# Four places instead of two for the split parts of queries and keys in a fused two-layer transformer kernel

## The reference, cut to what matters

```
xh = x[:, :, :DH];  x1 = layernorm(xh + mha(xh, wq1, ...), g1, be1)
xs = holt(x, 0.1, 0.1); x2 = layernorm(xs[:, :, :DH] + mha(xs[:, :, :DH], wq2, ...), g2, be2)
q = x @ wq.T + bq;  k = x @ wk.T + bk;  v = x @ wv.T + bv      # 8 heads of 8
a = softmax(q k^T / sqrt(8));  o = a v
```

## Time and profile before

| what | value |
|---|---|
| time, median of 3 runs | 2137.68 us (2133.76 to 2138.3) |
| profiled execution | 2140.73 us, span of its trace 2138.9 us |
| TensorE busy | 1884.9 us, 88% of the span |
| VectorE busy | 1776.4 us, 83% |
| ScalarE busy | 1444.4 us, 68% |
| GpSimd busy | 344.0 us, 16% |
| first `lead` (block 0) starts | 47.77 us |
| `lead` of blocks 2 to 7 starts | 62.86, 72.05, 81.15, 90.26, 99.48, 108.59 us |
| L730 starts | 117.37 us |
| first row maximum (L758) starts | 139.84 us |

### The profile page before, as it was taken

The page is one execution under the profiler, slowest core; times in us unless marked ns, Lnnn a source line. Parts: engine busy times, 40 slices in busy tenths (PEclk is TensorE's granted clock), DMA queues, the critical chain, the costliest instruction groups (busy, mean ns, idle before and its releaser), DMA issues.

```text
span 2138.9 us, 33478 instructions
## 1 busy us (share of the span) xinstructions
PE 1884.9 (88%) x11734; PEld 719.9 (34%) x11734; DVE 1776.4 (83%) x2689; ACT 1444.4 (68%) x2807; POOL 344.0 (16%) x516
## 2 busy tenths in 40 slices
PE   7537999999999999999999999988997887599884
PEld 6201222222222222222222222216764444266563
DVE  6689999999999999999999999903347887478778
ACT  5204888888888888888888888883322344567542
POOL 1210000000000222222222222000027652000000
PEclk9656999999999999999999999999998889799896
DMA  3231121120010111111111111016754332321321
GB/s 84 83 116 44 46 71 65 47 84 26 25 35 24 40 46 36 46 42 35 51 38 38 49 37 49 8 32 178 205 162 123 108 112 73 101 71 54 101 76 30
DMA packets 145888, 144.01 MB, mean 67 GB/s; under 512 B 29451, under 2 KB 124687, under 8 KB 145572
## 3 DMA queue, kind: packets, MB, share of 16 engines
q1 hardware_dynamic: 137380, 124.71, 19.2%
q0 software_dynamic: 8352, 17.29, 2.7%
HBM read 81.06 MB, written 60.03 MB: 66 GB/s over the span
## 4 chain that ended last, share of the span: by engine, by line
PE 70%; DVE 14%; ACT 8%; issue 3%; DMA 2%; SPq 2%; POOL 1%; DVEq 0%; ACTq 0%
PE PS L1606 23%; PE PS L1633 18%; PE PS L1588 8%; DVE mxp L758 6%; PE PS L1680 3%; ACT probs L1202 3%; ACT SG L1187 2%; PE PS L1736 2%; PE PS L1836 2%; PE PS L1854 1%; PE PS L1667 1%; PE PS L1745 1%; PE PS L1857 1%; PE PS L1839 1%; DMA xs_d<-SG 1%
## 5 line engine op out<-in xcount | busy, mean ns | idle before, releaser
L758 DVE TENSOR_REDUCE mxp<-PS 128x1 f32<-128x1024 f32 x1024 | 1203.5, 1220 | 43.9 <-PE PS L1588 29.2
L1202 ACT ACTIVATE probs<-PS 128x512 f32<-128x512 f32 x2048 | 1061.7, 604 | 168.1 <-PE PS L1633 164.9
L1633 PE MATMUL PS<-stacks 51*128 51x512 bf16 x2048 | 615.8, 383 | 28.2 <-ACT probs L1202 16.8
L1588 PE MATMUL PS<-stacks 48*128 48x512 bf16 x2048 | 518.9, 393 | 49.1 <-DVE mxp L758 30.4
L1606 PE MATMUL PS<-probs,VH 128*32 128x512 f32 x4096 | 546.7, 606 | 6.8 <-ACT SG L1187 6.1
L1633 PEld LDWEIGHTS PS<-stacks 51*128 51x128 bf16 x2048 | 154.3, 94 | 681.1 <-ACT probs L1202 611.7
L1588 PEld LDWEIGHTS PS<-stacks 48*128 48x128 bf16 x2048 | 109.5, 94 | 217.0 <-DVE mxp L758 178.0
L1472 POOL DMA_INDIRECT xe_d<-xn_s,rows_s x128 | 126.0, 984 | 328.5 <-PE PS L1606 292.6
L1497 POOL DMA_INDIRECT VP<-oe_d,ROWI x128 | 133.4, 1042 | 255.7 <-DMA oe_d<-stacks 194.7
L771 DVE TENSOR_TENSOR stacks<-stacks,PS 128x640 f32<-128x640 f32 x32 | 26.2, 820 | 134.7 <-ACT stacks L1234 134.7
L1606 PEld LDWEIGHTS PS<-probs,VH 128*32 128x32 f32 x4096 | 81.6, 108 | 125.0 <-issue 109.2
(11 more groups left out here) (344 smaller groups left out, 1922.4 us busy)
## 6 DMA issues: line engine op xcount, KB each, us to landing
xe_d<-zt SPq DMA_DIRECT2D x16, 640.0 KB
stacks<-xe_d SPq DMA_DIRECT2D x32, 320.0 KB, 3.3
oe_d<-stacks SPq DMA_DIRECT2D x32, 320.0 KB, 2.4
o_d<-SG SPq DMA_DIRECT2D x256, 32.0 KB, 1.6
ews<-in_ew_dram SPq DMA_DIRECT2D x33, 192.0 KB, 2.3
stacks<-ql_d SPq DMA_DIRECT2D x64, 96.0 KB
stacks<-kl_d SPq DMA_DIRECT2D x64, 96.0 KB
probs<-xs_d SPq DMA_DIRECT2D x18, 256.0 KB, 3.7
```

The source lines that it names most:

```text
L758: v.tensor_reduce(mxp[:, n // 2, n % 2:n % 2 + 1], MXB[n % 2].rearrange("p a c -> p (a c)"), X_AX, ALU.max).then_inc(mx_done, 1)
L1202: act.activation(probs[:, at:at + 512], PS[:, bank_of(u, e), :], ACT.Exp, scale=float(1.0 / np.sqrt(np.float32(DK)))).then_inc(exp_done, 1)
L1588: mm = pe.matmul(MXB[n % 2][:, i, :], QS[w][o:o + MAXROWS, (n // 2) * P:(n // 2 + 1) * P], KS[w][o:o + MAXROWS, key:key + 512], start=True ...
L1633: pe.matmul(PS[:, bank_of(u, e), :], KS[w][o:o + KROWS + 3, kt * P:(kt + 1) * P], QS[w][o:o + KROWS + 3, q0:q0 + 512], start=True, stop=Tr ...
```

## The change

The parts get four places in turn. Places 0 and 1 are those of before. Places 2 and 3 lie in QS[1], QS[2] and QS[3], the operand room of the attention's units 1 to 3, into which loads go only after the stores of parts have landed. `lead(j)` waits for the stores of block j-4. QREST, KREST and the PSUM banks keep their two places, and the order of every engine's list is as before.

```
         def part(parts, level, w):
-            return parts[level][:, w * 512:(w + 1) * 512]
+            if w < 2:
+                return parts[level][:, w * 512:(w + 1) * 512]
+            return QS[1 + level][:, ((parts is KPARTS) * 2 + w - 2) * 512:((parts is KPARTS) * 2 + w - 1) * 512]
...
-                        sp.dma_start(parts[lv, :, j * 512:(j + 1) * 512], part(src, lv, j % 2)).then_inc(stored, 16)
+                        sp.dma_start(parts[lv, :, j * 512:(j + 1) * 512], part(src, lv, j % 4)).then_inc(stored, 16)
...
-                    ins = v.scalar_tensor_tensor(left[w], PS[:, 4 + 2 * w + n, :], bcol[:, n:n + 1], part(parts, 0, w), ALU.add, ALU.subtract)
+                    ins = v.scalar_tensor_tensor(left[w], PS[:, 4 + 2 * w + n, :], bcol[:, n:n + 1], part(parts, 0, j % 4), ALU.add, ALU.subtract)
...
             def lead(j):
                 act.wait_ge(qk_ready, j + 1)
-                after(act, ql_st, 48 * (j - 1))
-                after(act, kl_st, 48 * (j - 1))
+                after(act, ql_st, 48 * (j - 3))
+                after(act, kl_st, 48 * (j - 3))
                 for n, parts in enumerate((QPARTS, KPARTS)):
-                    ins = act.activation(part(parts, 0, j % 2), PS[:, 4 + 2 * (j % 2) + n, :], ACT.Identity, bias=bcol[:, n:n + 1])
+                    ins = act.activation(part(parts, 0, j % 4), PS[:, 4 + 2 * (j % 2) + n, :], ACT.Identity, bias=bcol[:, n:n + 1])
...
-                    ins = act.activation(part(parts, 1, j % 2), left[j % 2], ACT.Copy)
+                    ins = act.activation(part(parts, 1, j % 4), left[j % 2], ACT.Copy)
...
-                    ins = pool.tensor_tensor(part(parts, 2, j % 2), left[j % 2], part(parts, 1, j % 2), ALU.subtract)
+                    ins = pool.tensor_tensor(part(parts, 2, j % 4), left[j % 2], part(parts, 1, j % 4), ALU.subtract)
```

## The result

The changed kernel takes 2118.92 us (median of 4 runs, 2117.65 to 2120.41), the kernel before 2137.99 us beside it (4 runs). The ratio is 0.991, 95% interval 0.9897 to 0.9924: 19.1 us faster. Forecast were 2118.9 us and a gain of 18.8. The profiled execution took 2120.41 us, its span is 2118.5 us. The insertion moved the lines behind it by two: L677 is now L679, L1606 is L1608.

A forecast was written before the change was run, and what follows sets the result against it. The front was taken as bound by lead's waits for stores, 9.11 us a block; with VectorE's list and its clashes setting the pace, L730 moves from 117.37 to 98.6, so 2137.7 - 18.8 = 2118.9 us, range 2111 to 2128.

The forecast's parts named there:

- The limit before: Front: a serial round through lead, middle, GpSimd and store landing, 9.11 us a block; VectorE waits 20.2 us for lead.
- What is late next: Front after the change: VectorE's list, below some 5.7 us a block, should run without a wait; other rounds need less.
- The clash: GpSimd meeting VectorE's experts' work: gaps of 4.07 us behind odd, 4.60 behind even blocks, and 0.5 lost on L721.
- The rule of the Trainium skill's page: Two-input VectorE and SBUF-reading GpSimd instructions exclude each other: odd gaps 4.3 us, L721 waiting 1.1, gain 17.5.
- The sum: Front: remainders, gaps and ranks() of 5.94 us put L730 at 98.6 instead of 117.37, a gain of 18.8 us.
- The loads: Attention's start: first load near 102.3 instead of 121.72, first scores near 116.5, 3.9 us of cover staying.
- Behind the front: After the first maximum at 121.1: every wait is on work that moves along, so the end gains 18.8 us too.
- the rival of e8: Behind the first maximum: the change shortens this part, 1999 us or more before, near 1996 changed; no chance given.
- C: Front: places not the limit, another round holds the pace near 9 us; gain at most 3.9, 2134 to 2138; chance 0.06.
- D: Attention: TensorE's full clock comes much later; 100 us of it makes the kernel 9 us slower, 2147; chance 0.05.
- A: Front: little or no clash of GpSimd with VectorE; gain 23 to 26, 2112 to 2115 us; chance 0.13.
- B: Front: more clash of GpSimd with VectorE on each block; gain 10 to 14, 2124 to 2128 us; chance 0.14.

The follow-up runs named there:

- e1: Changed kernel with four places, but lead(j) still waits for the stores of block j-2 as before; 2138.72 us, ratio to the kernel before 1.000.
- e3: Changed kernel with GpSimd's work on blocks 0 to 6 held back to lie under the next remainder and the reduction; 2112.78 us, ratio 0.9874.
- e2: Changed kernel with three places instead of four, lead(j) waiting for the stores of block j-3; 2119.87 us, ratio 0.9916.
- e4: Changed kernel with the marks and the two constant matrices of ranks() in bf16; 2117.45 us, ratio 0.9903.
- e8: The kernel before, unchanged, traced again on the third chip; 2230.42 us, ratio 0.9998.
- e10: The changed kernel, unaltered, run a third time, on the third chip; 2211.87 us, ratio 0.9905.
- e7: The changed kernel, unaltered, run again on the second chip; 2213.15 us, ratio 0.9914.
- e9: Changed kernel with the edits of e3 and e4, plus GpSimd's values instructions waiting for rows_done; third chip, 2205.45 us, ratio 0.990.

## Why the prediction was right

**The limit before.** Right, and shown by e1: with the old wait alone the gain is gone.

**What is late next.** Right: VectorE's list runs from 51.7 us to L723's end without a wait, and e3, with a shorter list, still has none before a remainder. So the other rounds were below it; what each of them takes was not measured. e2 agrees for the stores: the 9.11 us over two blocks, 4.6, also lie below the 5.66 that VectorE needs.

**The clash.** The taken values were 4.07 and 4.60 us for the gaps, and both were met to 0.01 us. That L721 would be hit was right too, with 0.83 us instead of 0.5. The rule of the Trainium skill's page "SBUF — State Buffer", section "Who interferes with whom", fits here: L716 and L720 have two SBUF inputs, L716 comes after GpSimd's first instruction and ends behind it, and in e3, with GpSimd elsewhere, the loss is gone. My estimate from it, a wait of 1.1 us, was too long: 0.84 is lost on L716 and 0.83 on L723. What I took from the page speaks of two SBUF inputs only, and the mark, L723, has one; that it loses as much is what the trace shows. The estimate's gain of 17.5 us is also by how much the first maximum moved, but by chance: its clashes were too long by 1.0 us in all, and the later start of the front (0.23) and the longer `ranks()` (0.70) made up for it.

**The sum.** L732 was forecast for 98.6 and came at 99.89. The 1.3 us are three terms: the front had started 0.23 us later (57.63 for 57.40), L723 cost 0.33 more, and `ranks()` took 6.64 us instead of 5.94. I had held it to the old length and named only a shorter one. The granted clock was at the low level (0.50 from 93 to 99 us, 1.2 GHz), where the mean over the 6 us of the old one was 0.64. In the five traces of fp32 `ranks()` with the new wait it took 5.3 to 6.8 us, so a term that I held fixed scatters by more than the whole miss of the sum.

**The loads.** Forecast 102.3 for the first load and 116.5 for the first scores, measured 102.77 and 117.02. The cover, from the first scores to the first maximum, was 5.3 us and not the 3.9 I had said would stay: the forecast's own 121.1 - 116.5 already gives 4.6.

**Behind the front.** The first maximum came 17.5 us earlier, not 18.8. The median gained 19.1 and the two profiled spans differ by 20.4. So 1.6 us of the median's gain are not the front's. The attention is the same in all traces: its last L1606 starts 1304.9 us behind the first maximum in the kernel before, 1305.2 in the changed one, 1304.7 to 1305.8 in the ten others. From the first maximum to the end of the span, attention included, it is 1999.1 us before and 1997.3 in e1, 1996.2 in the changed kernel, 1996.0, 1995.5 and 1995.5 in e2, e3 and e4. The last expert matmul starts 1444.6 to 1445.8 us behind the first maximum in all of these, and the differences arise behind it.

On the third chip this part, from the first maximum to the end of the span, is 2096.4 us before (e8) and 2090.2 after (e10), on the second 2093.0 after (e7), where the kernel before has no trace. So the rival of e8 is not refuted: the traces with the old wait have the longest rest. But e8's traced execution was 7.6 us above its median. If the trace's first maximum is subtracted from the median time instead, the rest is 1998.2 and 1999.4 us with the old wait and 1996.6 to 1998.0 with the new one in the first comparison and e1 to e4, but 2091.0 (e8) against 2090.4 and 2092.9 (e10, e9) on the third chip. Whether a fixed 1 or 2 us is among it stays open. The forecast of the median, met to 0.1 us, was thus closer than its parts, and that was luck: a front 1.3 us too optimistic, and a rest that gave about as much.

**Rivals.** C is out by the waits, D by the windows (the rise comes at the same distance from the first maximum, to 1 us, and the last L1606 too). A and B would have needed gaps of 3.2 or 5.5 us behind the odd blocks, against 4.07 measured. That the two engines always lose something where they meet, as I said against A, is too strong: in e3 the remainder, the reduction and GpSimd's two instructions lie beside each other, all at their undisturbed lengths.

## What to carry to other kernels

When a buffer's second use waits for a store, write down the whole round from one use to the next and divide it by the number of buffers; one more is enough as soon as the quotient falls below the busiest list (here three would have done). Then look at what the freed work will run beside: one VectorE instruction in each block lost 0.83 us to GpSimd here, and a wait that moved GpSimd under the remainder (one input from PSUM) and the reduction, which lost nothing beside it, gave 6 us more. Go by the durations in the trace and not by the number of SBUF inputs alone: the mark and a small copy have one each and lost 0.8 and 1.0 us.

## What was not expected

- A copy of 32 columns, 0.18 us alone, took 1.15 us beside GpSimd's subtraction (e4): a tiny instruction loses as much as a large one.
- `lead` waited 12.0 us for DMA in e2 with no effect on the time.
- The same kernel takes 2118.9 us in the first comparison and 2213.2 and 2211.9 on two other chips, with a front of the same length to 1.5 us and an attention to 0.4; the 93 to 94 us come after the experts. Why was not examined.
